# Graph layers on one core: a second one-hot gather in every second chunk

## What is computed

```python
# layer 0, per edge e: eight spline weights B[e, k], product of three fractions
z   = B[:, :, None] * x[src][:, None, :]          # [E, 8, 64]
agg = segment_sum(z.reshape(E, 512) @ W, dst)     # [N, 64]
y   = batchnorm(agg / count + x @ root);  x1 = layernorm(x + elu(y))
# layer 1
agg = segment_sum(x1[src] + edge_feats, dst)
out = layernorm(x1 + batchnorm(relu(agg @ W1 + b1) @ W2 + b2))
```

## Time and profile before

| what | us |
|---|---|
| median of three runs | 587.08 |
| profiled execution | 590.23 |
| its span, first to last instruction | 588.4 |
| TensorE busy | 513.9 |
| VectorE busy | 408.3 |
| ScalarE busy | 368.0 |
| GpSimd busy | 362.9 |
| mean granted clock of TensorE | 0.880 of full |

### The profile page before, as it was taken

One profiled execution on the slowest core, in us unless ns is written; L12 is line 12 of the kernel. 1 busy time (PEld: TensorE's weight loads), 2 busy tenths in 40 slices (PEclk: granted clock), 3 DMA queues, 4 the chain that ended last, 5 costly groups with the idle time before them and its releaser, 6 DMA issues.

```text
span 588.4 us, 13973 instructions
## 1 busy us (share of the span) xinstructions
PE 513.9 (87%) x4151; PEld 408.0 (69%) x4151; DVE 408.3 (69%) x1624; ACT 368.0 (63%) x662; POOL 362.9 (62%) x382
## 2 busy tenths in 40 slices
PE   4278997999999979879979988999899997799993
PEld 2267786888788868768768777887688886344532
DVE  6985787587777757657647663776756644979875
ACT  7585886688888867867867874885332332540154
POOL 6777777777777777777777777777777740000000
PEclk9977998799999989989989996999655556699997
DMA  7633445355454445434445443553252110000002
GB/s 146 144 75 72 104 111 118 74 122 122 120 124 109 108 99 121 102 95 122 97 99 120 97 109 68 119 123 67 63 107 52 26 19 3 0 1 1 2 1 54
DMA packets 89144, 48.75 MB, mean 83 GB/s; under 512 B 76252, under 2 KB 77667, under 8 KB 89069
## 3 DMA queue, kind: packets, MB, share of 16 engines
q1 hardware_dynamic: 75949, 35.40, 25.7%
q0 software_dynamic: 11968, 12.28, 10.6%
q10 hardware_dynamic: 1152, 0.16, 0.2%
HBM read 46.86 MB, written 0.93 MB: 81 GB/s over the span
## 4 chain that ended last, share of the span: by engine, by line
PE 49%; DMA 16%; ACT 11%; DVE 10%; POOL 6%; issue 6%; ACTq 1%; DVEq 1%; SPq 0%; POOLq 0%
PE ps L676 10%; DMA u<-codes_scratch 9%; PE ps L595 9%; PE ps L635 8%; ACT u L983 7%; DMA rows<-in_x,idx 6%; POOL rows L524 6%; PE ps L855 6%; PE ps L620 5%; ACT adj L996 3%; PE ps L860 2%; PE ps L614 2%; PE ps L603 1%; DVE pair L1290 1%; PE ps L710 1%
## 5 line engine op out<-in xcount | busy, mean ns | idle before, releaser
L524 POOL DMA_INDIRECT rows<-in_x,idx x374 | 361.6, 967 | 115.8 <-issue 100.9
L676 PE MATMUL ps<-whot_room,rows 128*128 128x96 f32 x816 | 182.0, 309 | 19.6 <-DMA rows<-in_x,idx 16.7
L983 ACT ACTIVATE u<-u,own 128x768 uint8<-128x768 uint8 (+1 forms) x168 | 152.4, 957 | 38.9 <-DMA u<-codes_scratch 38.8
L595 PE MATMUL ps<-pair,ohp 128*125 128x300 bf16 (+1 forms) x416 | 151.0, 366 | 29.0 <-ACT adj L996 15.2
L996 ACT CAST adj<-ps 125x500 f32 x208 | 122.7, 590 | 78.3 <-PE ps L603 64.4
L676 PEld LDWEIGHTS ps<-whot_room,rows 128*128 128x128 f32 x816 | 143.0, 217 | 29.2 <-issue 17.4
L1290 DVE TENSOR_SCALAR pair<-iota_h,comb 128x300 bf16<-128x300 int16 (+1 forms) x416 | 103.3, 311 | 49.7 <-PE ps L603 46.0
L635 PE MATMUL ps<-xs,u 125*128 125x192 bf16 x1050 | 136.0, 255 | 0.5 <-DVE rows L1341 0.4
L1294 DVE TENSOR_SCALAR ohp<-iota_h,srcp 128x125 bf16<-128x125 int16 x416 | 110.0, 277 | 1.3 <-issue 1.3
L1305 DVE TENSOR_TENSOR agg<-agg,ps 128x24 f32 x416 | 75.3, 181 | 44.1 <-PE ps L620 38.5
L635 PEld LDWEIGHTS ps<-xs,u 125*128 125x128 fp8e4 x1050 | 94.8, 105 | 9.6 <-issue 0.5
(11 more groups left out here) (209 smaller groups left out, 383.9 us busy)
## 6 DMA issues: line engine op xcount, KB each, us to landing
u<-codes_scratch SPq DMA_DIRECT2D x42, 400.0 KB, 4.1
rows<-in_edge_attr SPq DMA_DIRECT2D x51, 256.0 KB
rows<-in_x,idx POOLq DMA_INDIRECT x374
x_now<-in_x SPq DMA_DIRECT2D x25, 31.2 KB
adj<-in_x SPq DMA_DIRECT2D x1, 700.0 KB
xs<-in_x SPq DMA_DIRECT2D x1, 700.0 KB
out<-u SPq DMA_DIRECT2D x3, 224.0 KB
adj<-in_edge_attr SPq DMA_DIRECT2D x1, 576.0 KB
```

Of the source, the lines that this page charges most:

```text
L524: pool.indirect_dma_start(rows[:, s, t, 0:C], None, x, bass.IndirectOffsetOnAxis(ap=idx[:, at:at + 1], axis=0)).then_inc(gathered[0][0] if ...
L595: return nc.tensor.matmul(m_ps[0:PN, bank_of(g), 0:PAIRS].rearrange("p (j w) -> p j w", w=GWIN)[:, :, low:low + WIDTHS[n]], ohp[:, par, t, ...
L676: last = nc.tensor.matmul(z_ps[:, half, at:at + ZW], rows[:, s, t, :], whot[:, par, t, :], start=True, stop=True)
L983: last = nc.scalar.activation(of, of, ACT.Abs_reciprocal_sqrt, bias=own[:, 0:1], scale=SHARP)
```

## The change

Chunks 6, 8, ... 44 (`is_more`, 20 of them) have a second tile taken, t = 6: 354 tiles are gathered in place of 374. The codes table gets 20 more lines. A new buffer `more_codes` holds the second tile's line, loaded by SyncE (`load_more`). It is VectorE, not ScalarE, that turns it into one-hots, in place and in five pieces of 640 (`make_more`): each element is compared with `own_code`, a column that lies in PSUM. It does this at the end of every odd chunk from 3 to 41, three chunks ahead. The 25 products (`take_more`) are split: 12 at t = 5 and 6 of an even chunk, 13 at t = 1 to 3 of the next. The first taken tile's 25 then go to t = 1 to 3 of the even chunk and t = 5 and 6 of the odd one. Both use the one bank `taken_ps`, so each waits until VectorE has kept the other (`keep_taken`, `keep_more`).

The source one-hots of four tiles are now built by one operation that compares a row of numbers in PSUM (`iota_q`) with `srcp` spread out (`build_nodes`, 128x500), two a chunk in place of eight `build_node`. The pair one-hots are interleaved with the windows. Some semaphores are merged, and the counter `begun`, which nothing read, is gone.

```diff
@@ -86,7 +86,28 @@
     PARTS = 3
     HOTS = NT * P
     SHARP = 16384.0
-    SHARES = {t: range(NT * (t - 1) // 6, NT * t // 6) for t in range(1, 7)}
+    MORE_FROM = TAKE_FROM + 3
+    MORES = (TAKE_TO - MORE_FROM + 1) // 2
+    ROWS = TAKES + MORES
+    MORE_SPLIT = NT // 2
+    def spread_over(js, tiles):
+        return {t: js[len(js) * n // len(tiles):len(js) * (n + 1) // len(tiles)] for n, t in enumerate(tiles)}
+    def is_more(c):
+        return MORE_FROM <= c < TAKE_TO and c % STEP == 0
+    def takes_of(c):
+        return (TAKE_FROM <= c < TAKE_TO) + is_more(c)
+    def shares_of(c):
+        if c % STEP == 0 and is_more(c + 2):
+            return spread_over(range(NT), range(1, 4)), spread_over(range(MORE_SPLIT), range(5, 7))
+        if c % STEP == 1 and is_more(c + 1):
+            return spread_over(range(NT), range(5, 7)), spread_over(range(MORE_SPLIT, NT), range(1, 4))
+        return spread_over(range(NT), range(1, 7)), {}
+    MORE_PIECES = [range(j, j + 5) for j in range(0, NT, 5)]
     PIECES = (range(0, 7), range(7, 13), range(13, 19), range(19, NT))
     HIGH_BITS = -0x0F0F0F10
...
@@ -237,7 +260,9 @@
         sum_banks = ps[:, 2:6, :]
         hot = ps[:, 6, 0:RW].rearrange("p (t w) -> p t w", w=WIN)
-        iota_p = ps[:, 6, RW:RW + WIN]
+        iota_q = ps[:, 6, RW:RW + PN]
+        iota_p = iota_q[:, 0:WIN]
+        own_code = ps[:, 6, RW + PN:RW + PN + 1]
         missed_ps = ps[0:1, 3, 2 * RW + C:2 * RW + C + 1]
         xt_ps, xroot_ps = ps[0:C, 2, 2 * RW:2 * RW + PN], ps[0:PN, 3, 2 * RW:2 * RW + C]
...
@@ -419,12 +444,17 @@
             def load_x(n):
                 sp.wait_ge(xt_turned, n)
-                sp.sem_inc(begun, 1)
                 sp.dma_start(x_now[:, :], x[bass.ds(n * PN, PN), :]).then_inc(x_copied, 16)
             def load_codes(c, par):
                 sp.dma_start(codes[par], codes_dram[bass.ds(c - TAKE_FROM, 1), :].to_broadcast([P, HOTS])
                              ).then_inc(codes_loaded[par], 16)
+            def load_more(n):
+                if n > 0:
+                    sp.wait_ge(more_taken, n)
+                sp.dma_start(more_codes[:, :], codes_dram[TAKES + n:TAKES + n + 1, :].to_broadcast([P, HOTS])
+                             ).then_inc(more_loaded, 16)
             for s in range(SLOTS):
                 load_ea(s, s)
...
@@ -527,15 +557,15 @@
                             gathered[0][0] if last and CH // 2 <= t < CH - STEP else gathered[s][t // (CH // 2)], 16)
             for c in range(SLOTS):
-                gather_chunk(0, c, in_step=False, one_taken=(c >= TAKE_FROM))
+                gather_chunk(0, c, in_step=False)
             for c in range(SLOTS, NCH):
-                gather_chunk(c // AHEAD, c % AHEAD, last=(c == NCH - 1), one_taken=(c < TAKE_TO))
+                gather_chunk(c // AHEAD, c % AHEAD, last=(c == NCH - 1))
             def gather_again(of, layer):
                 with pool.Fori(0, T) as t:
                     pool.wait_ge(fb_idx_ready[layer], t + 1)
                     pool.wait_ge(fb_added[layer], t * NR + 1)
-                    pool.sem_inc(begun, 1)
+                    pool.sem_inc(pool_step, 1)
                     pool.indirect_dma_start(
                         rows[:, 0, 0, 0:C], None, of,
                         bass.IndirectOffsetOnAxis(ap=fb_idx[:, 0:1], axis=0)).then_inc(fb_fetched[layer], 16)
...
@@ -625,26 +655,34 @@
                 return nc.tensor.matmul(sums_of(slice(0, C), par, RW, ts), upper_halves(ones[:, 0:C]),
                                         upper_halves(hot_of)[:, ts, 0:WIN], start=True, stop=True)
-            def take_rows(c, par, t):
-                if t == min(SHARES):
+            def take_rows(c, par, js):
+                if js[0] == 0:
                     pe.wait_ge(hots_ready, c - (TAKE_FROM - 1))
-                    if not isinstance(c, int) or c > TAKE_FROM:
+                    if c > TAKE_FROM:
                         pe.wait_ge(taken_kept, c - TAKE_FROM)
-                    pe.sem_inc(begun, 1)
-                for j in SHARES[t]:
+                    if is_more(c):
+                        pe.wait_ge(more_kept, (c - MORE_FROM) // STEP + 1)
+                for j in js:
                     last = nc.tensor.matmul(taken_ps, hots[par][:, j * P:(j + 1) * P], xs[0:PN, j, :],
                                             start=(j == 0), stop=(j == NT - 1))
-                if t == max(SHARES):
+                if js[-1] == NT - 1:
                     last.then_inc(taken, 1)
-            def second_half(i, c, s):
-                if isinstance(c, int):
-                    return sum(16 * (CH // 2 - (TAKE_FROM <= n < TAKE_TO)) for n in range(s, c + 1, SLOTS))
-                return i * (GATHERED - 16) + (GATHERED - 16 * (s >= TAKE_FROM))
+            def take_more(n, js):
+                if js[0] == 0:
+                    pe.wait_ge(more_ready, n + 1)
+                    pe.wait_ge(taken_kept, MORE_FROM + n * STEP - TAKE_FROM)
+                for j in js:
+                    last = nc.tensor.matmul(taken_ps, more_hots[:, j * P:(j + 1) * P], xs[0:PN, j, :],
+                                            start=(j == 0), stop=(j == NT - 1))
+                if js[-1] == NT - 1:
+                    last.then_inc(more_taken, 1)
+            def second_half(c, s):
+                return sum(16 * (CH // 2 - takes_of(n)) for n in range(s, c + 1, SLOTS))
             pe.wait_ge(weights_loaded, 48)
-            pe.wait_ge(kernels_ready, D)
+            pe.wait_ge(basis_in, 1 + D)
             pe.wait_ge(t_ready, 2)
             count_pairs(0, 0, 0, 0)
             count_pairs(0, 0, 1, 0).then_inc(m_ready, 1)
...
@@ -662,14 +701,18 @@
                     if n == GROUP - 1:
                         carry_over(c, g, par, bank_of(g + 1))
                     half = t // (CH // 2)
-                    if takes_next and t in SHARES:
-                        take_rows(i * SLOTS + (s + 1), prev, t)
+                    if takes_next and t in shares:
+                        take_rows(c + 1, prev, shares[t])
+                    if takes_next and t in more_shares:
+                        take_more((c + 2 - par - MORE_FROM) // STEP, more_shares[t])
                     if t == 0:
                         pe.wait_ge(ea_loaded[s], i * 16 + 16)
                         pe.wait_ge(whot_ready, c + 1)
                     if t % (CH // 2) == 0:
-                        pe.wait_ge(gathered[s][half], second_half(i, c, s) if half else i * GATHERED + GATHERED)
+                        pe.wait_ge(gathered[s][half], second_half(c, s) if half else i * GATHERED + GATHERED)
                         pe.wait_ge(zsb_ready, c * 2 + (half + 1))
+                    if is_more(c) and t == TAKEN - 1:
+                        pe.wait_ge(more_kept, (c - MORE_FROM) // STEP + 1)
                     if one_taken and t == TAKEN:
                         pe.wait_ge(taken_kept, c - (TAKE_FROM - 1))
                     at = (t % (CH // 2)) * ZW
...
@@ -1285,16 +1330,15 @@
                                                                ).to_broadcast([P, CH, KIN, WIN]),
                     ALU.mult).then_inc(whot_ready, 1)
-            def build_pairs(c, par, half):
-                for t in range(half * CH // 2, (half + 1) * CH // 2):
-                    nc.vector.tensor_scalar(hots_of_pairs(par, t // GROUP, t % GROUP), iota_h[:, 0:NT * WIDTHS[t % GROUP]],
-                                            comb[:, bass.ds(c * CH + t, 1)], None, ALU.is_equal)
-            def build_node(c, par, t):
-                one_hot = nc.vector.tensor_scalar(ohp[:, par, t, :], iota_h[:, 0:PN], srcp[:, bass.ds(c * CH + t, 1)],
-                                                  None, ALU.is_equal)
-                if t % (CH // 2) == CH // 2 - 1:
-                    one_hot.then_inc(oh_ready, 1)
+            def build_pair(c, par, t):
+                nc.vector.tensor_scalar(hots_of_pairs(par, t // GROUP, t % GROUP), iota_h[:, 0:NT * WIDTHS[t % GROUP]],
+                                        comb[:, bass.ds(c * CH + t, 1)], None, ALU.is_equal)
+            def build_nodes(c, par, half):
+                first, n = half * CH // 2, CH // 2
+                nc.vector.tensor_tensor(
+                    ohp[:, par, first:first + n, :], iota_q.rearrange("p (a q) -> p a q", a=1).to_broadcast([P, n, PN]),
+                    each(srcp[:, bass.ds(c * CH + first, n)], PN), ALU.is_equal).then_inc(oh_ready, 1)
             def starts_of(c, ts):
                 return [dve.value_load(bass.AP(base, offset=c * CH + t, ap=[[T, 1], [1, 1]])) for t in ts]
...
@@ -1341,6 +1386,20 @@
                 nc.vector.tensor_reduce(
                     bass.AP(rows, offset=slot * (CH * P) + TAKEN * P, ap=[[SLOTS * CH * P, P], [1, C]]),
                     taken_ps.rearrange("p (n c) -> p c n", n=PARTS), AX.X, ALU.add).then_inc(taken_kept, 1)
+            def make_more(n):
+                dve.wait_ge(more_loaded, n * 16 + 16)
```

(30 more changed lines are left out.)

58 lines of the change are left out of this document (32 added, 26 removed).

## The result

The changed kernel takes 635.2 us (median of 4, 632.3 to 641.9) where the kernel before takes 588.9 beside it: a ratio of 1.077 [1.068, 1.086]. It is **slower by 46 us**; I had said no change.

A forecast was written before the change was run, and what follows sets the result against it. GpSimd's gathers were taken to pace the main loop, with TensorE to become the bound. Main loop +27, tail -24.3 and last chunk -2.7 on 590.2 gave 590 us profiled, 587 us as median; range 570 to 612.

The forecast's parts named there:

- My estimate from the page: VectorE's pieces by the skill page: 0.82 us per 640 columns, a wait of 1.1 us, 11 us more in sum.
- The checks: Behind make_more of chunks 3, 5 and 7: a longer VectorE chain and falling clock cost 17.5 us together.
- the wait's size: Even chunk's t = 5: VectorE's chain of 7.2 us against TensorE's 6.7, a wait of 0.5 us a pair.
- TensorE's own pair: Main loop at full clock: 15.55 - 0.58 + 2.06 = 17.0 us a pair; with the VectorE wait 17.55.
- the chain is dearer: Rival, VectorE's pieces: 0.82 us each gives 597; 1 us each gives 1.9 us wait a pair, 614; chance 0.13.
- The tail: Chunk 44's sums to the last chunk's: 46.3 us at full clock against 70.6, 24 us less.
- the rival to which I gave 0.25: Tail: one early wait drops the clock, which without takes does not come back; tail 70 us, total 611; 0.25.
- the saving that I had forecast for the last chunk: The last chunk's products, some 5.6 us at half clock before, save another 2.7 us.
- GpSimd's 25 us: GpSimd: 20 gathers less at 1.25 us save 25 us, in full only if TensorE can follow.
- the 41 us of products: TensorE, main loop: 25 more products a pair, 2.06 us, make 41 us over 20 pairs, all on its path.

The follow-up runs named there:

- the loads ahead: The changed kernel, but VectorE loads all four registers of a half's windows ahead of its wait, none between keep and pairs: 600.9 us, 1.024 of the kernel before.
- the four edits: Changed kernel with register loads ahead of VectorE's wait, two of five pieces mid even chunk, pieces compared with an SBUF scalar, second tiles from chunk 12: 573.9 us, 0.980.
- one small piece: The changed kernel, but VectorE makes one 128-column operation instead of five of 640 per second tile, whose rows are left out of the result: 576.7 us, 0.986.
- two pieces later: The changed kernel, but VectorE makes two of each second tile's five pieces later, in the middle of the even chunk: 592.6 us, 1.013.

## Why the prediction was wrong

**What held.** TensorE takes over as the bound and GpSimd waits for it. The takes are 0.08 us apart. The wait stands where I put it, for the keep that I named, with 3.65 us of pieces and 0.59 for 500 columns. By an estimate from the Trainium skill, *VectorE: DVE Perf Modes*, the errata's formula (stated there for fp32 additions), a piece lasts 0.82 us, and the trace agrees: 0.81 on the mean. My estimate from the page took that for their distance, which is 0.73 us, as in the forecast: the next one starts before the last has ended. The same page says in "The DRAIN you can't avoid" that an operation which is not held starts earlier, and I had left that out.

The checks came out near in sum: chunk 4's to chunk 10's sums took 71.6 us, and the forecast had 69. Their waits, in chunks 6 and 8, were 5.4 and 7.2 us where I had 3.4 and 6.2:

```profile
99.71 1.11 PE L676 MATMUL ps<-xs,more_codes 125*128 125x192 bf16 x6 [5.37 <-DVE rows L1386]
...
121.56 0.48 PE L625 MATMUL ps<-pair,ohp 128*125 128x300 bf16 x1 [7.16 <-ACT adj L1041]
```

**What failed first: the wait's size.** I had 7.2 - 6.7 = 0.5 us. It is 8.24 - 6.36 = 1.9 between the two rows, 1.81 by the step. Of the 1.3 us that were missing, 0.86 are the register loads that the new order leaves bare. I added up the operations that the trace names, and register loads aren't among its busy rows; in the kernel before they stand behind four pair one-hots in a row, which cover them. The order of the program showed them directly behind the keep. The run with the loads ahead puts them at 0.88 us. Another 0.3 is TensorE's, which comes after 6.36 us and not 6.7. I had taken off the 0.16 us that the kernel before shows as a wait for ScalarE's copy, but the products right behind it are slower too; why, no run shows. From 196.58 to 197.40 they take 0.82 us; at the same place after the change, without the wait, 0.59. First the kernel before, then the changed one:

```profile
196.58 0.34 PE L595 MATMUL ps<-pair,ohp 128*125 128x300 bf16 x1 [0.16 <-ACT adj L996]
...
197.40 0.49 PE L635 MATMUL ps<-xs,u 125*128 125x192 bf16 x4
```

```profile
254.69 0.34 PE L625 MATMUL ps<-pair,ohp 128*125 128x300 bf16 x1
...
255.28 0.84 PE L666 MATMUL ps<-xs,u 125*128 125x192 bf16 x8
```

These waits are almost all gone, and TensorE's own pair is 16.45 us, not 17.0. The rest is the time from the keep's start to the products, 0.50 in the rows where I had 0.36. The lighter pair half paid the wait back: 16.45 + 1.81 = 18.26 against 17.55, which is 0.7 x 17 = 12 us of the 28.

**What was missing: the clock.** I priced the wait at its length. A fall of the clock behind it adds 1.2 to 1.9 us, 17 us over 11 of 17 pairs; the short last step takes 1.5 off, and that is the rest of the 28. I had looked at the fall behind 3.2 us and taken it as the point where falls begin, though the 1.44 us wait of the earlier trace rows stood in my own rows. The rival "the chain is dearer" named 1.9 us of wait and "perhaps a falling clock", but hung it on slower pieces, the wrong term, and gave it 0.13.

**The tail** was forecast at 46.3 us and took 60.3. The clock was full through chunks 45 and 46 (6.70 and 5.65 us), and then came the rival to which I gave 0.25: a single wait of 1.6 us, after which half clock stays, here for at least 38 us. I had seen no wait since I looked for late gathers; at full clock TensorE overtakes VectorE's early sums, which was no limit while it ran at half.

That a fallen clock does not come back without takes, as the rival had it, is not so in general. The other traces have the same wait ahead of the second fold, 1.4 to 1.8 us, except where the fold was moved or the clock was already at half. With the four edits the clock fell behind it and was back 20 us later; with one small piece it was back after some 7 us; with two pieces later it did not fall there at all. First the four edits, then two pieces later:

```profile
426.00:446.00 20.00, 20.00 (x108) 17.44 (x108) 12.31 (x45) 5.46 (x11) 15.14 (x16) 0.51 0.52 89
446.00:456.00 10.00, 9.71 (x84) 8.46 (x82) 8.37 (x38) 5.02 (x11) 7.54 (x8) 0.97 0.16 29
```

```profile
436.00:443.00 7.00, 6.42 (x61) 5.84 (x61) 3.61 (x16) 2.52 (x6) 5.34 (x6) 1.00 1.07 191
```

So the wait is shown, and what decides how long half clock lasts is open.

Together: 28 in the main loop's pairs, 2.6 at the checks, 14 in the tail, 2.6 at the start and 4.6 behind chunk 51 make 51.8, and 641.9 - 590 is 51.9. The start is 2.6 us longer in the run without a second tile as well, and chunk 4's sums come anywhere from 67.0 to 73.0 us in the variants' profiles, so it may be scatter. Of the 4.6, 2.7 are the saving that I had forecast for the last chunk: the clock was still at half there (0.50 from 528 to 536 us). The other 1.9 I didn't test.

**And where did GpSimd's 25 us go?** With VectorE out of the way the main loop is 340.4 us, as before (340.3): the 41 us of products on TensorE eat the gain. What is left of it is the tail, 70.6 down to 51.4 us, and to 52.6 with the four edits.
